# Windowed attention scores: each head contracted over its own 64 rows, two heads on the two halves of the PE array

## The reference

```
for i in range(DEPTH):                                     # 6
    x = attn_layer(shift_tokens(x), Wqkv[i], q_scale[i], k_scale[i], Wo[i]) + x
    x = ffn_layer(shift_tokens(x), ...) + x
# attn_layer: 16 heads of 64; q, k = l2norm * scale, rotary with xpos scale
# local_attention: windows of 32 queries against 64 keys (the window before and its own)
sim  = jnp.einsum('bhwie,bhwje->bhwij', bq, bk2) * QK_SCALE    # contracts e = 64
attn = jax.nn.softmax(jnp.where(mask, -big, sim), -1)
out  = jnp.einsum('bhwij,bhwje->bhwie', attn, bv2)
```

## Time and profile before

| what | value |
|---|---|
| median of 3 runs | 3474.66 us (3468.48 to 3475.24) |
| span of the profiled execution | 3463.4 us |
| the median less this span | 11.3 us |
| PE busy | 3295.0 us, 95% of the span |
| DVE busy | 2841.0 us, 82% |
| POOL busy | 2637.8 us, 76% |
| ACT busy | 1825.1 us, 53% |

### The profile page before, as it was taken

One profiled execution on the slowest core, in us unless ns is written; L12 is line 12 of the kernel. 1 busy time (PEld: TensorE's weight loads), 2 busy tenths in 40 slices (PEclk: granted clock), 3 DMA queues, 4 the chain that ended last, 5 costly groups with the idle time before them and its releaser, 6 DMA issues.

```text
span 3463.4 us, 71935 instructions
## 1 busy us (share of the span) xinstructions
PE 3295.0 (95%) x27964; PEld 1634.9 (47%) x27964; DVE 2841.0 (82%) x3289; ACT 1825.1 (53%) x2684; POOL 2637.8 (76%) x1918
## 2 busy tenths in 40 slices
PE   6899976899999999999999999999999999999987
PEld 4333333454545454555545454555555454555443
DVE  6899937888888888888888888888888888888863
ACT  2578843455454555555454555555454555555442
POOL 3223228988888888888888888888888888888860
PEclk7899988999999999999999999999999999999999
DMA  6333133333333333333323333323333233333331
GB/s 211 81 61 64 37 103 78 74 74 74 81 73 83 77 72 72 85 81 75 80 68 77 76 85 78 72 70 86 81 73 79 71 77 76 86 75 74 74 75 30
DMA packets 178111, 270.05 MB, mean 78 GB/s; under 512 B 42480, under 2 KB 67056, under 8 KB 176112
## 3 DMA queue, kind: packets, MB, share of 16 engines
q1 hardware_dynamic: 174032, 251.03, 30.0%
q10 hardware_dynamic: 3744, 14.43, 1.2%
HBM read 44.43 MB, written 19.55 MB: 18 GB/s over the span
## 4 chain that ended last, share of the span: by engine, by line
PE 65%; DVE 5%; POOL 5%; SPq 4%; ACT 4%; issue 1%; DMA 1%; POOLq 0%; DVEq 0%; ACTq 0%
PE ly_to_ps L1061 19%; PE ly_pj_ps L980 14%; PE ly_pair_ps L1029 8%; PE ly_pair_ps L1049 7%; SPq L906 4%; PE ly_pair_ps L1078 4%; PE ly_to_ps L1085 4%; DVE ly_prod L1165 3%; ACT ly_u L1339 3%; PE ly_pair_ps L1018 2%; PE ly_nq_ps L990 2%; DMA ly_kbd<-ly_kr 1%; PE ly_pair_ps L1038 1%; POOL ly_kr L1412 1%; POOL ly_kr L1411 1%
## 5 line engine op out<-in xcount | busy, mean ns | idle before, releaser
L1165 DVE SCALAR_TENSOR_TENSOR ly_prod<-ly_pj_ps,ly_few,ly_tables 128x1024 f32<-128x1024 f32 x768 | 964.6, 1272 | 189.7 <-ACT ly_sq L1308 171.6
L1308 ACT ACTIVATE ly_sq<-ly_pj_ps 128x512 f32<-128x512 f32 x768 | 451.1, 602 | 745.6 <-PE ly_pj_ps L980 701.9
L980 PE MATMUL ly_pj_ps<-ly_xs,ly_wqk 128*128 128x512 f32 x1536 | 795.1, 615 | 34.2 <-DVE ly_prod L1165 21.8
L1061 PE MATMUL ly_to_ps<-ly_u,ly_mvo 128*128 128x512 f32 x1536 | 720.6, 598 | 0.2 <-DVE x_all L1238 0.2
L1417 POOL TENSOR_TENSOR ly_sq<-ly_sq 128x512 f32<-128x512 f32 x384 | 490.7, 1278 | 229.1 <-ACT ly_sq L1308 228.7
L1339 ACT COPY ly_u<-ly_pair_ps 128x1024 f32<-128x1024 f32 x384 | 378.7, 1013 | 239.0 <-PE ly_pair_ps L1049 239.0
L1421 POOL TENSOR_TENSOR ly_sx<-ly_sx,ly_smax 128x1024 f32<-128x1024 f32 x192 | 365.4, 1903 | 145.1 <-DVE ly_smax L1205 145.1
L980 PEld LDWEIGHTS ly_pj_ps<-ly_xs,ly_wqk 128*128 128x128 f32 x1536 | 268.8, 191 | 426.2 <-issue 291.5
L1061 PEld LDWEIGHTS ly_to_ps<-ly_u,ly_mvo 128*128 128x128 f32 x1536 | 277.1, 190 | 287.2 <-issue 287.2
L1049 PE MATMUL ly_pair_ps<-ly_pt,ly_xt 32*128 32x512 f32 x3072 | 383.9, 613 | 20.0 <-ACT ly_u L1339 13.0
L1029 PE MATMUL ly_pair_ps<-ly_kbd,ly_qp 128*32 128x128 f32 x12288 | 376.0, 276 | 24.2 <-DMA ly_kbd<-ly_kr 21.0
(11 more groups left out here) (122 smaller groups left out, 4351.8 us busy)
## 6 DMA issues: line engine op xcount, KB each, us to landing
ly_qp<-ly_qr SPq DMA_DIRECT2D x768, 128.0 KB, 2.3
ly_kbd<-ly_kr SPq DMA_DIRECT2D x1536, 64.0 KB, 2.0
ga_parts_dram<-ga_parts SPq DMA_DIRECT2D x16, 384.0 KB, 2.5
ga_qs<-ga_parts_dram SPq DMA_DIRECT2D x96, 64.0 KB
ga_ks<-ga_parts_dram SPq DMA_DIRECT2D x96, 64.0 KB
ly_wqk<-in_wqk SPq DMA_DIRECT2D x24, 256.0 KB, 3.4
ly_mvo<-mvo_dram SPq DMA_DIRECT2D x6, 1024.0 KB, 6.5
mvo_dram<-ga_pt ACTq DMA_DIRECT2D x4, 1024.0 KB, 6.1
```

Of the source, the lines that this page charges most:

```text
L980: pe.matmul(pj_ps[:, j % 2, :], wqk[:, g, j % TILES, :], xs[:, n % 2, WIN:], start=True, stop=True).then_inc(proj_ready.sem, 1)
L1061: last = pe.matmul(to_ps[:], mvo[:, h, :], u[:, :, :, h, :].rearrange("p t c q -> p (t c) q"), start=(h == 0), stop=(h == LH - 1))
L1165: dve.scalar_tensor_tensor(prod[:, k], pj_ps[:, j % 2, :].unsqueeze(1).to_broadcast([P, 2, N]), gains[:, n // B, k:k + 1], tables[:, table ...
L1308: act.activation(sq[:, k, :], pj_ps[:, j % 2, :], ACT.Square).then_inc(sq_done.sem, 1)
```

## The change

The queries' and keys' rows are regrouped so that one head of a pair lies on rows 0 to 63 and the other on rows 64 to 127. The keys need no zero blocks then (`kbd` becomes `kp`, half the size). Each matmul of 128 rows and 128 moving columns becomes two of 64 rows and 64 moving columns, one for each head, on the two row halves of the array, into two PSUM banks. The number of score matmuls doubles. Queries are copied in 8 DMAs of 32 partitions instead of 4 of 64; keys still take 8. The scores now come out in the order head, block of tokens instead of block, head, so the layouts of `sx`, `smax`, `rsum` and the access patterns of their users change. Inside a unit the second and third head trade places for the queries (`BESIDE`), which the table `heads` and `combine` take into account.

```diff
+BESIDE = (0, 2, 1, 3)
-        kbd = sb("kbd", [P, 2, 2, 2, WIN + N])
-        sx = sb("sx", [P, 2, T, 4, SPAN])
+        kp = sb("kp", [P, 2, 2, WIN + N])
+        sx = sb("sx", [P, 2, 4, T, SPAN])
...
-                for p in range(2):
-                    for half in range(2):
-                        sp.dma_start(qp[64 * half:64 * half + 64, g, p], qr[64 * p:64 * p + 64, half]).then_inc(qp_loaded.sem, 16)
+                for p in range(2):
+                    for z in range(2):
+                        for half in range(2):
+                            src, dst = 64 * p + 32 * z, 64 * z + 32 * half
+                            sp.dma_start(qp[dst:dst + 32, g, p], qr[src:src + 32, half]).then_inc(qp_loaded.sem, 16)
...
-                            src, dst = 64 * p + 32 * z, 64 * half + 32 * z
-                            sp.dma_start(kbd[dst:dst + 32, g % 2, p, z, WIN:], kr[src:src + 32, g, half]).then_inc(kbd_loaded[g % 2].sem, 16)
+                            src, dst = 64 * p + 32 * z, 64 * z + 32 * half
+                            sp.dma_start(kp[dst:dst + 32, g % 2, p, WIN:], kr[src:src + 32, g, half]).then_inc(kp_loaded[g % 2].sem, 16)
...
-                for t in range(T):
-                    for p in range(2):
-                        for c in range(4):
-                            w, at = 4 * t + c, 256 * (t % 2) + 128 * p
-                            last = pe.matmul(pair_ps[32 * c:32 * c + 32, k, t // 2, at:at + 128], qp[:, g, p, WIN * w:WIN * w + WIN],
-                                             kbd[:, g % 2, p, :, WIN * w:WIN * w + SPAN], start=True, stop=True, skip_group_check=True)
+                for p in range(2):
+                    for t in range(T):
+                        for c in range(4):
+                            for z in range(2):
+                                w, at, rows = 4 * t + c, SPAN * (T * p + t), slice(64 * z, 64 * z + 64)
+                                last = pe.matmul(pair_ps[32 * c:32 * c + 32, k, z, at:at + SPAN], qp[rows, g, p, WIN * w:WIN * w + WIN],
+                                                 kp[rows, g % 2, p, WIN * w:WIN * w + SPAN], start=True, stop=True, skip_group_check=True)
...
-                    last = pe.matmul(to_ps[:], mvo[:, h, :], u[:, :, :, h, :].rearrange("p t c q -> p (t c) q"), start=(h == 0), stop=(h == LH - 1))
+                    last = pe.matmul(to_ps[:], mvo[:, 4 * (h // 4) + BESIDE[h % 4], :], u[:, :, :, h, :].rearrange("p t c q -> p (t c) q"), start=(h == 0), stop=(h == LH - 1))
...
-                dve.tensor_tensor(sx[:, g % 2], pair_ps[:, where["scores", n, g]].rearrange("p b (t h k) -> p (b t) h k", h=4, k=SPAN),
-                                  mask[:].unsqueeze(2).to_broadcast([P, T, 4, SPAN]), ALU.add).then_inc(s_masked.sem, 1)
+                dve.tensor_tensor(sx[:, g % 2], pair_ps[:, where["scores", n, g]].rearrange("p z (h t k) -> p (z h) t k", t=T, k=SPAN),
+                                  mask[:].unsqueeze(1).to_broadcast([P, 4, T, SPAN]), ALU.add).then_inc(s_masked.sem, 1)
...
-                dve.transpose(pt[:, :, 4 * g:4 * g + 4].rearrange("p t h k q -> p t (h k q)"),
-                              sx[:, g % 2].rearrange("p t h k -> p t (h k)")).then_inc(pt_done.sem, 1)
+                dve.transpose(pt[:, :, 4 * g:4 * g + 4].rearrange("p t h k q -> p h t (k q)"), sx[:, g % 2]).then_inc(pt_done.sem, 1)
```

More of the change, by code:

```diff
@@ L782, in layers_part @@
         kr = sb("kr", [P, UNITS, 2, N])
-        kbd = sb("kbd", [P, 2, 2, 2, WIN + N])
-        sx = sb("sx", [P, 2, T, 4, SPAN])
-        smax = sb("smax", [P, 2, T, 4])
-        rsum = sb("rsum", [P, 2, T, 4])
+        kp = sb("kp", [P, 2, 2, WIN + N])
+        sx = sb("sx", [P, 2, 4, T, SPAN])
+        smax = sb("smax", [P, 2, 4, T])
+        rsum = sb("rsum", [P, 2, 4, T])
         pt = sb("pt", [P, T, LH, 2, WIN])
@@ L800, in layers_part @@
         pair_ps = ps("pair_ps", [P, 2, 2, N])
-        early, consts, xs_set, kbd_set = (sem(x) for x in ("early", "consts", "xs_set", "kbd_set"))
+        early, consts, xs_set, kp_set = (sem(x) for x in ("early", "consts", "xs_set", "kp_set"))
         wqk_loaded = [tally(f"wqk_loaded_{g}", 16) for g in range(UNITS)]
@@ L812, in layers_part @@
         rot_done = tally("rot_done", 4 * UNITS)
-        qp_loaded = tally("qp_loaded", 16 * 4 * UNITS)
+        qp_loaded = tally("qp_loaded", 16 * 8 * UNITS)
         ns_ready = tally("ns_ready", UNITS)
@@ L820, in layers_part @@
         keys_done = tally("keys_done", UNITS)
-        kbd_loaded = [tally(f"kbd_loaded_{k}", 16 * 8 * UNITS // 2) for k in range(2)]
+        kp_loaded = [tally(f"kp_loaded_{k}", 16 * 8 * UNITS // 2) for k in range(2)]
         s_ready = tally("s_ready", UNITS)
@@ L887, in _ @@
             load_up(0)
-            sp.wait_ge(kbd_set, 1)
+            sp.wait_ge(kp_set, 1)
             def queries(n, g):
@@ L1154, in _ @@
             dve.memset(xs[:], 0.0).then_inc(xs_set, 1)
-            dve.memset(kbd[:], 0.0).then_inc(kbd_set, 1)
+            dve.memset(kp[:], 0.0).then_inc(kp_set, 1)
             dve.wait_ge(early, 32)
@@ L1404, in rotate @@
                     if n:
-                        pool.wait_ge(kbd_loaded[g % 2].sem, kbd_loaded[g % 2].at(n - 1, 16 * 8 * (g // 2 + 1)))
+                        pool.wait_ge(kp_loaded[g % 2].sem, kp_loaded[g % 2].at(n - 1, 16 * 8 * (g // 2 + 1)))
                 else:
@@ L1408, in rotate @@
                     if UNITS * n + g:
-                        pool.wait_ge(qp_loaded.sem, 16 * 4 * (UNITS * n + g))
+                        pool.wait_ge(qp_loaded.sem, 16 * 8 * (UNITS * n + g))
                 low, high = prod[:, 2 * side], prod[:, 2 * side + 1]
@@ L1420, in less_max @@
                 pool.wait_ge(s_max.sem, s_max.at(n, g + 1))
-                pool.tensor_tensor(sx[:, g % 2], sx[:, g % 2], smax[:, g % 2].unsqueeze(3).to_broadcast([P, T, 4, SPAN]),
+                pool.tensor_tensor(sx[:, g % 2], sx[:, g % 2], smax[:, g % 2].unsqueeze(3).to_broadcast([P, 4, T, SPAN]),
                                    ALU.subtract).then_inc(s_less.sem, 1)
             def scale_scores(n, g):
-                rq = rn[:, n % 2, 0:NSUM].rearrange("p (t r) -> p t r", t=T)[:, :, 4 * g:4 * g + 4]
+                rq = rn[:, n % 2, 0:NSUM].rearrange("p (t r) -> p r t", t=T)[:, 4 * g:4 * g + 4]
                 pool.wait_ge(steps.sem, steps.at(n, STEPS))
                 pool.wait_ge(s_less.sem, s_less.at(n, g + 1))
-                pool.tensor_tensor(sx[:, g % 2], sx[:, g % 2], rq.unsqueeze(3).to_broadcast([P, T, 4, SPAN]),
+                pool.tensor_tensor(sx[:, g % 2], sx[:, g % 2], rq.unsqueeze(3).to_broadcast([P, 4, T, SPAN]),
                                    ALU.mult).then_inc(s_scaled.sem, 1)
@@ L1432, in normal_probs @@
                 pool.wait_ge(p_sum.sem, p_sum.at(n, 2 * g + 2))
-                pool.tensor_tensor(sx[:, g % 2], sx[:, g % 2], rsum[:, g % 2].unsqueeze(3).to_broadcast([P, T, 4, SPAN]),
+                pool.tensor_tensor(sx[:, g % 2], sx[:, g % 2], rsum[:, g % 2].unsqueeze(3).to_broadcast([P, 4, T, SPAN]),
                                    ALU.mult).then_inc(p_ready.sem, 1)
@@ L1503, in constants @@
         for side in range(2):
-            heads[p, g, side, LH * side + 4 * g + p // HALF] = 1
+            heads[p, g, side, LH * side + 4 * g + (p // HALF if side else np.array(BESIDE)[p // HALF])] = 1
     eps = np.zeros((P, NRN), np.float32)
```

4 lines of the change are left out of this document (2 added, 2 removed).

## The result

The changed kernel takes **3558.03 us** (median of 4 runs, 3556.93 to 3566.7) against 3471.57 (3466.07 to 3475.24) for the kernel before: ratio 1.0256 [1.0237, 1.0276]. It is slower by 86 us where 76 less were forecast, and lies outside the range.

The account below looks back on a forecast made before the run. PE was taken to bound the kernel, with DVE capping its gain of 2.31 us an item (3 x 0.85 - 0.24) at 1.7. 46 x 1.7 = 78 us, less 2 for SP's queue: 3474.7 - 76 = 3398 us, range 3368 to 3475.

Parts of the forecast that it names:

- What a score matmul costs: Score units on PE: 128 matmuls on eight tiles take 0.92 us with the first weight load, 0.85 us saved a unit.
- instructions arrive slower than the tiles want: Rival, score units: 5 to 6.5 ns an instruction, a unit 1.3 to 1.65 us, total time 3420 to 3470 us; chance 0.15.
- turns of the halves: Rival, score matmuls: row halves of one column group alternate, a unit 1.79 us, total time 3488 us; chance 0.12.
- Eight tiles at once: Score units: two row halves times four column groups all stream at once, saving 0.85 us a unit.
- Switches of 0.12 us each: PE, scores 0 and 3 into square_sums: new tiling switches cost 0 to 0.22 us each, 0.12 taken, 0.24 an item.
- DVE as the cap: DVE, gated product to product 4: limits PE's gain of 2.31 us an item to 1.7.
- Layouts at nothing: DVE, ACT and POOL: same element counts, runs of 64 elements or more, so new access patterns cost nothing.
- SP's queue: Query DMAs, 8 instead of 4 a unit: at most 0.15 us wait an item; 0 to 10 us at the ends, 2 taken.
- The 11.3 us: Whole kernel: the median lies this far above the profiled span, so forecast span 3387 and median 3398 us.
- a unit above 1.3 us: Sign that the forecast is wrong, in score units: slow arrival of instructions or turns.
- DVE's higher share: Sign that the forecast is right: DVE's busy share at 84%, its wait before the feed-forward sum gone.
- the item of 57.9 us: Sign that the forecast is right: an item takes 57.9 us, from 59.64 before.

Follow-up runs that it names:

- 32 DMAs, scores last: Changed kernel with a head's rows interleaved, 32 key and query DMAs an item, PE order scores 2, down, scores 3, square_sums 3: 3434.05 us, 0.9909.
- four kernels shown: Changed kernel 3558.03 us; kernel before with score matmuls cut into 64 columns 3579.95; changed kernel with both heads on rows 0 to 63 3662.18; interleaved rows, old order 3529.88.
- 32 DMAs and the burst: Changed kernel with interleaved rows, 32 DMAs an item, and its own PE order scores 2, scores 3, square_sums 3, down: 3529.88 us, 1.0183.
- the scores last: Changed kernel, 64 DMAs an item, PE order scores 2, down, scores 3, square_sums 3: 3469.03 us, 1.0006; the kernel before in that order: 3470.83 us.
- small-stages-apart order: Changed kernel, 8 query DMAs, combine 14 between scores 0 and square_sums 0, end order scores 2, down, scores 3, token_transposes, square_sums 3: 3524.32 us, 1.0168.
- both heads on one row half: Changed kernel with both heads' score matmuls on rows 0 to 63, the second half of the array unused: 3662.18 us (two executions), 1.0557.
- cut columns: Kernel before with each 128-row score matmul cut into two of 64 moving columns, old layouts and DMAs: 3579.95 us, 1.0328.

## Why the prediction was wrong

**The step that failed** is in "What a score matmul costs": the rate at which instructions arrive was taken from a restart of 12 instructions in 0.09 us, and "I take 0.92, because that row is a start from standstill and therefore no steady rate". The restart row does show that a few instructions can go fast, and the traces show how many: in all 138 units of the fastest kernel (32 DMAs, scores last) that have no wait inside and run at full clock, the 32nd matmul starts 0.24 us after the first, 7.7 ns a pair, near the 7 ns forecast for eight tiles. From the 33rd on the median is 10.5 ns a pair (11.6 in the same order with 64 DMAs). So 64 instructions go at the pace of the tiles, and the other 192 of the unit don't. Two things stood in place of the 0.92 us:

- *The unit.* It takes 1.41 to 1.69 us, 11 to 13 ns a pair of load and matmul instead of 7. The rival "instructions arrive slower than the tiles want" (1.3 to 1.65 us) had the right size, and its chance of 0.15 was too small. The gain is 0.1 to 0.35 us a unit. Over an item of the changed kernel the scores had 84 / 44.5 = 1.9 us of new waits and were only 1.0 us longer, so the four units gained 0.9 us, 0.22 each, where 0.85 was forecast. It isn't turns of the halves, and it is hardly the tiles themselves: the same tiles take the first 32 pairs of each unit at 7.7 ns. That speaks for the supply of instructions, but no run varies the supply alone.
- *The burst.* No term of the sum was a standstill: the forecast put the wait for instructions at nothing and cost scores 2 and 3 as two units. Together they are 512 instructions, the restart comes 3.5 to 4.0 us after the burst's start in all four kernels shown, and what the burst doesn't fill of that time is a stall: in the items shown 0.8 to 1.0 us where its matmuls are slow, 1.7 to 2.3 where they are fast. This is why faster matmuls brought nothing at this place: each tenth that the unit saves, the stall takes back. The kernel before has 256 instructions in 3.6 us at this place, and only 11.1 us of waiting.

The Trainium skill, Advanced Engine Details and Errata, ISA Cache, says that an engine's instructions come in lines of 16 KB, 256 instructions, and that it holds only two of them. The trace agrees with the line: 16.4 KB a packet. It gives TensorE a memory of 128 KB all the same, in which the whole burst would fit; the stalls of this trace speak for the two lines.

**Point by point.**
- *Eight tiles at once:* right as a mechanism (1.42 to 1.52 against 1.99 us on one half), but the unit saves 0.1 to 0.35 us and not 0.85.
- *Switches of 0.12 us each:* right. Their price is at the end of the unit. With 32 DMAs and the burst, a unit that runs straight into the next one takes 1.28 us (median of 45) and one that runs into square_sums 1.41 (median of 45); in the kernel before both take 1.77. square_sums itself took 0.57 us at full clock, as before (0.55). With the scores last it has a mean of 2.54 us an item against 2.26 in the kernel before; of these 13 us in all, 6.3 are waits on "issue" in front of it. That the earlier unit had used up its instructions was my guess, and the run made for it failed.
- *DVE as the cap:* never reached, so neither shown nor refuted. DVE's busy time in the stretch fell from 2331 to 2261 us with the slower items.
- *Layouts at nothing:* right. DVE's mask has a mean of 1210 ns, 1213 before; POOL's scaling of the scores 1934 ns instead of 1903, 0.1 us an item.
- *SP's queue:* 16 DMAs an item more were put at 0 to 10 us, 2 taken. They cost 0 to 10 us with the burst and 11.5 without it, and another 16 key DMAs less were worth 23 (3457.5 to 3434.1). The cost per DMA was right (0.63 us); that only lateness of a transfer counts was not, since units got shorter too.
- *Clock:* had no term. Behind the stalls it fell to 0.50, which cost square_sums 0.44 us and down mostly 0.6 to 1.7 each time, some 17 us together over the 11 items of the 32 (0.7 an item) that these two stages lost. Another 9.8 us are waits on "issue" in front of square_sums.
- *The 11.3 us* between median and profiled span are not a fixed part. Each later execution is some 2 us longer than its own span (3558.66 against 3556.6); the rest fits the spread between executions (3466.07 to 3475.24). The forecast doesn't hang on it, since it takes the 76 us off the median.
- *Of the signs named ahead,* "a unit above 1.3 us" came, DVE's higher share and the item of 57.9 us didn't. PE idle before scores 3 on the DMA of the keys (22.1 us) came too and was misleading: with it gone, PE waited for instructions in the same burst.

**Not settled:** where in the timed runs the 11.5 us of the query DMAs lie, why the small-stages-apart order had more block waits, why a unit is faster with fewer DMAs, and when the clock falls behind a wait and when not. The profile names the block wait only "issue"; that it is one follows from its distance of whole blocks, from the q8 packets and from the runs with the burst apart.

## What to carry to other kernels

Count instructions, not only columns: cutting work into twice as many small ones pays up to the rate at which the engine is fed. In these kernels 256 instructions (128 pairs of load and matmul) that were used up in less than some 3.3 us ended in a wait for the next block, however fast the array could be. Put a stage of few and long instructions (here `down`, 6 matmuls in 2.8 us) between two such units; that alone was worth 89 us here (3558.0 to 3469.0), and 96 with half the DMAs. And where a sum doesn't care for the order of its rows, choose the order that lets one DMA do the work of two.

## What the hardware showed that was not expected

- With half the DMAs (32 an item), PE stands still for 1.7 to 2.3 us in a burst of 512 instructions, at a place that moves by 23 instructions from item to item. In four kernels it goes on 3.5 to 4.0 us after the burst's start, whether the matmuls before it took 11 or 16 ns each, and 1.1 to 1.6 us after a packet of 16 KB has come in on the instruction queue.
- The first 32 pairs of a unit with eight tiles go at 7.7 ns each, the others at 10.5 ns or more. A unit that leads into another tiling pays 0.13 us at its end.
- Behind such a stall the clock was at 0.50 and the six matmuls of `down` took 3.37 to 3.84 us in the two items shown, instead of 2.77. With both heads on one row half it fell 26 times in the 2740 us, with cut columns once, though the waits on "issue" above 0.5 us have a median of 1.1 us in both.
- A load and a matmul of 64 rows, 32 columns of weights and 64 moving columns go at 11.0 ns a pair with eight tiles (1.41 us / 128) and at 15.5 ns with four (1.99 us / 128).
- A DMA to every second partition is hardly slower: the page gives 2.4 us from issue to landing. The queries' DMAs of the kernel before, with the same bytes to 64 partitions in a row, had 2.3, the keys' with half the bytes 2.0:

```profile
ly_kp<-ly_kr SPq DMA_DIRECT2D x768, 128.0 KB, 2.4
```
